# A ViT tower on one core: class attention placed inside the last group's attention, class rows' FFN with its own buffers

## The chip, the cores and the metric

The kernel runs on one core of a Trainium2 chip. Its metric is the device time of one execution in microseconds (us). A core has TensorE (PE, matrix products and transposes, results into PSUM), VectorE (DVE), ScalarE (ACT), GpSimd (POOL) and SyncE (SP, which issues DMAs), each working through its own list of instructions in order; they wait for each other by semaphores.

## The reference

64 images of 3x224x224 become 64 patch tokens of width 128 and one class token each; then one layer of attention and a feed-forward network (FFN) with experts.

```python
tokens = jnp.einsum('bpi,hi->bph', patches, W) + b
h = jnp.concatenate([cls, tokens], axis=1) * pos_embed
# attention on layernorm(h), 8 heads of 16
q = relu(split_heads(x @ Wq.T + bq)); k = relu(split_heads(x @ Wk.T + bk)); v = split_heads(x @ Wv.T + bv)
attn = softmax(einsum('bhnd,bhmd->bhnm', q, k) / (k.sum(-1, keepdims=True) + 1e-6))
h = h + einsum('bhnm,bhmd->bhnd', attn, v) merged @ Wo.T + bo
# FFN on layernorm(h), normalised once more with ln_scale and ln_bias
a, b = split(flat @ shared_in_w.T, 2); out_shared = (silu(a) * b) @ shared_out_w.T + shared_out_b
h_expert = the same form with expert_in_w                      # one hidden vector for all experts
routed = sum over 8 experts of comb[:, e] * (h_expert @ expert_out_weight[e].T)   # group by argmax, top 2 of 4 by softmax
h = h + out_shared + routed
```

## The kernel before

The 64 images are worked in 8 groups of 8 (GROUPS = 8, L = 7 is the last); a group is 512 patch tokens, four tiles of 128. `groups(engine, body)` writes `body(g, par)` for each group on each engine, with a loop over the middle ones. In a body stand the attention of group g, the FFN of group g-1, and, except in the last two groups, the patch embedding of group g+2. The order of the work is written out by hand on each engine: nothing plans it. `need(engine, event, g)` waits until the event of group g has come.

Attention of a group goes in four parts p: `score(g, p)`, `row_maxes`, `exps`, `prob_transpose`, `probs_out`, `prob_v(g, p)`, `row_sums`; then `attn_scale`, `attn_sum`, `attn_transpose`, `attn_out`, `out_proj`, `residual`, `norm2`, `norm2_scale`, `z_transpose`, `z_out`. The FFN of a group goes: `gates`, `logits`, `ffn_in(g, k)` for k = 0 to 3 (k = 0, 1 the shared net, 2, 3 the expert net; each six matmuls of high and low parts), `silus`, `hidden_mul`, `choose` (top 2), `route_exp`, `weights`, `counts`, `shared_t`, `shared_natural`, `shared_add`, and the eight expert products `expert(g, u)`, which `weigh(g, u)` multiplies by the routing weights and GpSimd's `expert_sum` adds up; `output` is the last sum, `store` the DMA to memory. All 64 class tokens of the kernel are one more pass, called group 8 (GROUPS), of 64 rows.

The class tokens' attention over the patches is done once, in the last group: `class_scores`, `class_max`, the exponentials, `class_softmax`, `class_probs`, then `class_values(0)` and `(1)`, 32 matmuls of 8 columns each half, `class_own` and `class_out`. Before the change the value halves stand behind `out_proj` and `z_transpose` of group 7, in banks acc and O, and the class rows' FFN uses the patch rows' tiles (z_nat, z_hi, silu, hidden, comb), so its steps wait until group 7 has finished with them. Behind the last body each engine has a written-out tail with group 7's FFN and the class rows' FFN.

Two waits matter below. `ffn_in(g, 0)` waits for all eight weighings of group g-1, since both use bank C0; and `weigh(g, u)` for even u waits for an earlier `expert_sum`, since there are two product buffers for the four tiles:

```python
if half == 0:
    if t >= 2:
        need(dve, tree_done, g, t - 1)
    else:
        need(dve, tree_done, g - 1, t + 3)
```

## Time and profile before

| | |
|---|---|
| median of 3 runs | 537.16 us (536.97 to 537.72) |
| the profiled execution's own time | 538.47 us |
| its span | 536.6 us |
| TensorE busy | 489.3 us, 91% |
| VectorE, ScalarE, GpSimd busy | 321.2, 184.1, 173.8 us |
| mean granted clock of TensorE | 0.94 of full |

The span is the time between the first and the last instruction of the profiled execution. The views read are: the page; busy time and granted clock by stretch ("PEclk" 1.00 is 2.4 GHz, 0.50 is 1.2 GHz); the timeline of one engine, whose rows give start, duration, engine, line, operation, tiles and what ended an idle time before it; and the chain that ended last. The last group's body runs from about 424 us on, the written-out tail from about 486 us.

### The profile page before, as it was taken

Reading aid. Unit: us, or ns where it says so; the run is one execution under the profiler, and the core shown is the slowest. Engines: PE = TensorE matmul, PEld = TensorE weight load, DVE = VectorE, ACT = ScalarE, POOL = GpSimd, SP = SyncE. Lnnn points to the kernel's source line nnn. Section 1 sums busy time; section 2 is a strip of 40 time slices with the busy share of each in tenths; the row PEclk is TensorE's granted clock in tenths of the full one; section 3 lists DMA queues with packets and bytes.
Section 4 is the critical chain, followed back from the end, with each engine's and each line's share of the span. In section 5 each row is a group of like instructions: output and inputs, shape, how many; then the busy total and the mean of one; then the engine's idle time right before and its main releaser. Section 6 shows DMA issues by size and latency. Waiting matters only on the chain.

```text
span 536.6 us, 6981 instructions
## 1 busy us (share of the span) xinstructions
PE 489.3 (91%) x2194; PEld 331.9 (62%) x2194; DVE 321.2 (60%) x869; ACT 184.1 (34%) x342; POOL 173.8 (32%) x213
## 2 busy tenths in 40 slices
PE   5899997999999999999999999999697869898974
PEld 2355556665775578557755776567576646786562
DVE  0043356375856586658765776667677758646652
ACT  0035115432273218411742255215631553122220
POOL 6013201120462037202711183107311821224443
PEclk9989996899999999999999999999979978969976
DMA  8995660055004600461045200000100010000001
GB/s 340 352 410 188 203 223 0 0 177 184 1 20 165 197 1 6 136 200 41 0 136 164 79 0 20 0 0 1 21 0 1 1 21 0 1 1 1 20 1 22
DMA packets 14413, 44.71 MB, mean 83 GB/s; under 512 B 1721, under 2 KB 7090, under 8 KB 14386
## 3 DMA queue, kind: packets, MB, share of 16 engines
q1 hardware_dynamic: 12882, 42.39, 23.4%
q10 hardware_dynamic: 1504, 1.99, 1.1%
q8 instruction: 14, 0.23, 0.2%
q14 instruction: 13, 0.11, 0.1%
HBM read 42.24 MB, written 2.13 MB: 83 GB/s over the span
## 4 chain that ended last, share of the span: by engine, by line
PE 68%; DVE 15%; issue 7%; DMA 4%; POOL 3%; ACT 2%; ACTq 1%; DVEq 0%; POOLq 0%; SPq 0%
PE acc L421 20%; PE scores L482 6%; PE O L508 5%; PE B L407 4%; DMA bq_row<-in_bq_row 3%; DVE z_nat L1080 2%; PE scores L620 2%; PE C L620 2%; PE B L445 2%; PE C L621 1%; PE acc L655 1%; PE C L559 1%; PE C L622 1%; PE B L464 1%; PE scores L621 1%
## 5 line engine op out<-in xcount | busy, mean ns | idle before, releaser
L421 PE MATMUL acc<-x_main,w_patch 128*128 128x512 f32 x288 | 137.6, 607 | 5.9 <-DMA w_patch<-in_w_patch 5.9
L421 PEld LDWEIGHTS acc<-x_main,w_patch 128*128 128x128 f32 x288 | 53.2, 194 | 49.3 <-issue 41.4
L1567 POOL TENSOR_TENSOR prod<-prod 128x512 f32<-128x512 f32 (+1 forms) x33 | 42.6, 1292 | 35.2 <-DVE prod L1292 35.1
L839 ACT ACTIVATE probs<-shift 128x512 f32<-128x512 f32 x32 | 20.4, 637 | 80.8 <-DVE shift L1132 80.8
L508 PEld LDWEIGHTS O<-v_bd,probs_t 128*128 128x128 f32 x256 | 33.6, 200 | 22.7 <-issue 12.1
L1560 POOL TENSOR_TENSOR hidden_lo<-silu,hidden_hi 128x512 fp32r<-128x512 f32 (+1 forms) x18 | 20.9, 1164 | 74.8 <-ACT hidden_hi L839 74.7
L482 PE MATMUL scores<-k_bd,q_mask 128*128 128x260 f32 x128 | 38.4, 425 | 5.8 <-DVE shift L1132 3.1
L508 PE MATMUL O<-v_bd,probs_t 128*128 128x64 f32 (+1 forms) x256 | 35.6, 284 | 5.0 <-ACT probs_t L839 5.0
L1128 DVE TENSOR_REDUCE row_max<-scores 128x8 f32<-128x520 f32 x32 | 22.3, 698 | 28.8 <-PE scores L482 28.4
L482 PEld LDWEIGHTS scores<-k_bd,q_mask 128*128 128x128 f32 x128 | 23.3, 203 | 18.7 <-issue 7.9
L1529 POOL TENSOR_TENSOR p_cls<-exp_cls,row_rec 128x16 f32<-128x16 f32 x16 | 3.5, 222 | 94.0 <-DVE row_rec L1147 94.0
L839 ACT ACTIVATE probs_t<-B 128x512 f32<-128x512 f32 x32 | 19.0, 593 | 43.3 <-PE B L407 43.3
L620 PE MATMUL C<-w_eout_hi,hidden_hi 128*128 128x512 f32 (+1 forms) x66 | 30.5, 462 | 1.9 <-POOL hidden_lo L1560 0.7
L1292 DVE TENSOR_TENSOR prod<-scores,comb 128x512 f32<-128x512 f32 (+1 forms) x33 | 22.5, 683 | 15.8 <-POOL routed L1574 9.8
L620 PE MATMUL scores<-w_eout_hi,hidden_hi 128*128 128x512 f32 (+1 forms) x66 | 30.0, 454 | 0.2 <-DVE prod L1292 0.2
L1510 POOL TENSOR_TENSOR rstd<-var,neg_half 128x4 f32<-128x4 f32 x8 | 8.1, 1015 | 64.8 <-DVE var L1076 64.8
L1158 DVE TENSOR_TENSOR attn_patch<-O,row_rec 64x256 f32<-64x256 f32 x32 | 13.5, 422 | 25.4 <-PE O L508 24.9
L621 PE MATMUL C<-w_eout_lo,hidden_hi 128*128 128x512 f32 (+1 forms) x66 | 28.4, 430 | 0.0
L622 PE MATMUL C<-w_eout_hi,hidden_lo 128*128 128x512 f32 (+1 forms) x66 | 28.2, 428 | 0.0
L621 PE MATMUL scores<-w_eout_lo,hidden_hi 128*128 128x512 f32 (+1 forms) x66 | 27.7, 420 | 0.0
L622 PE MATMUL scores<-w_eout_hi,hidden_lo 128*128 128x512 f32 (+1 forms) x66 | 27.6, 418 | 0.0
L1292 DVE TENSOR_TENSOR prod<-C,comb 128x512 f32<-128x512 f32 (+1 forms) x33 | 22.0, 679 | 8.9 <-PE C L622 8.9
(251 smaller groups left out, 1016.7 us busy)
## 6 DMA issues: line engine op xcount, KB each, us to landing
x_main<-in_x_main SPq DMA_DIRECT2D x48, 768.0 KB, 4.2
out_tokens<-y_out SPq DMA_DIRECT2D x16, 128.0 KB, 2.5
w_patch<-in_w_patch ACTq DMA_DIRECT2D x6, 192.0 KB, 9.7
prod<-in_w_eout SPq DMA_DIRECT2D x2, 512.0 KB
x_tail<-in_x_tail SPq DMA_DIRECT2D x8, 96.0 KB, 3.3
silu<-in_w_in SPq DMA_DIRECT2D x2, 256.0 KB
hidden<-in_rows ACTq DMA_DIRECT2D x1, 256.0 KB, 16.1
w_attn<-in_w_attn ACTq DMA_DIRECT2D x1, 256.0 KB, 17.5
```

Source lines behind the costliest of these rows:

```text
L407: last = nc.tensor.transpose(dst[0:rows, t * 128:(t + 1) * 128], src, ident)
L421: last = mm(acc[:, :], w_patch[:, j, :], x_main[:, j, :], start=(j == 0), stop=False)
L482: last = mm(scores[:, b2, 0:HP * SEQ], q_mask[:, b, :, :].rearrange("p e n -> p (e n)"), k_bd[:, b, :, :].rearrange("p h m -> p (h m)"), s ...
L508: last = mm(O[:, c:c + 64].rearrange("p (b c) -> p b c", b=2), probs_t[p % 2][:, hp * 128:(hp + 1) * 128], pair, start=True, stop=True)
L620: mm(dst[0:rows, :], h_hi, w_hi, start=(c == 0), stop=False)
L621: mm(dst[0:rows, :], h_hi, w_lo, start=False, stop=False)
L622: last = mm(dst[0:rows, :], h_lo, w_hi, start=False, stop=(c == HC - 1))
L839: return nc.scalar.activation(dst, src, func, **kw)
L1128: v.tensor_reduce(row_max[p % 2][:, :, :], s, AX.X, ALU.max).then_inc(max_done.sem, 1)
L1292: v.tensor_tensor(prod[t % 2][0:rows, half, :].rearrange("p (e d) -> p e d", d=D), src[0:rows, :].rearrange("p (e d) -> p e d", d=D), bcas ...
L1560: q.tensor_tensor(hidden_lo[:, c, 0:n], silu[c][:, 0:n], hidden_hi[:, c, 0:n].bitcast(F32), ALU.subtract).then_inc(hlo_done.sem, 1)
L1567: q.tensor_tensor(p[r, 0, :], p[r, 0, :], p[r, 1, :], ALU.add).then_inc(tree1_done.sem, 1)
```

## The change

The class attention's steps move forward into the last group's attention: `class_max` ahead of `row_maxes(7, 0)`, `class_softmax` ahead of `row_sums(7, 0)`, `class_probs` behind `score(7, 2)`, `class_values(0)` behind `prob_transpose(7, 1)`, `class_values(1)` behind `score(7, 3)`, `class_out` ahead of `prob_v(7, 3)`. The second bank of the values is C0 and not O, for which `shared_t(6)` waits. The expert products of group 6, `counts(6)`, `shared_t(6)` move back accordingly. The class rows' second norm moves into the body, with tiles of its own (h2_cls, z_cls, zc_t, zc_hi, zc_lo, silu_cls, hidden_cls and its high and low part, comb_cls), which end the waits for the patch rows' tiles. In the tail the class FFN stands between group 7's steps, its two expert products go to banks O and acc, VectorE adds them up itself (`class_experts`), they stand ahead of the products 6 and 7 of group 7, and the class rows are stored ahead of group 7's. One of the three table loads of ScalarE in the tail is gone. GpSimd's sums 1 to 3 of group 6 move behind z_low(7) and between the steps of the tail. The memory set aside for DMA descriptors is made smaller, to fit the new tiles.

```diff
                 load_x(g)
-            for g in range(GROUPS - 5, GROUPS):
+            for g in range(GROUPS - 5, GROUPS - 1):
                 store(g)
 
-            need(sp, yout_done, GROUPS)
+            sp.wait_ge(tdve.sem, 22)
             sp.dma_start(out[:, 0, :], y_cls[0:IMAGES, 0:D]).then_inc(stored.sem, 16)
+            store(GROUPS - 1)
...
                 t, half = u // 2, u % 2
-                if u == 0:
+                if is_class(g):
+                    need(pe, hlo_done, g)
+                    need(pe, hid_done, g)
+                elif u == 0:
...
                     need(pe, prod_done, g, u - 3)
-                if isinstance(g, int) and g == GROUPS:
-                    need(pe, prod_done, g - 1)
-                dst = expert_bank(u)
+                dst = (O, acc)[u] if is_class(g) else expert_bank(u)
...
                 score(g, 2)
+                if not nxt:
+                    class_probs()
...
                 fill(9, 10)
-                if lean:
+                if not nxt:
+                    class_values(0)
+                elif lean:
                     expert(g - 1, 0, 128)
                 prob_v(g, 1)
+                score(g, 3)
                 if not nxt:
-                    class_probs()
-                score(g, 3)
+                    class_values(1)
...
                 fill(13, 14)
-                if lean:
+                if not nxt:
+                    expert(g - 1, 0, 128)
+                elif lean:
...
                 fill(18, NMAIN + 1)
-                if lean:
+                if not nxt:
+                    shared_t(g - 1, TOK)
+                    class_out()
+                elif lean:
...
                     to_natural(g + 1, 1 - par)
-                if lean:
+                if not nxt:
+                    shared_natural(g - 1, TILES, 128)
+                    expert(g - 1, 1, 128)
+                elif lean:
...
                     expert(g - 1, 1, 128)
+                if not nxt:
+                    expert(g - 1, 2, 128)
...
                     normed_t(g + 1)
-                else:
-                    class_values(0)
...
                     expert(g - 1, 4, 128)
+                if last:
+                    expert(g - 1, 5, 128)
+                if not nxt:
+                    expert(g - 1, 6, 128)
+                if last:
+                    z_transpose(g)
                 if nxt and last:
-                    expert(g - 1, 5, 128)
-                if last:
-                    z_transpose(g)
-                if not nxt:
-                    class_values(1)
-                    expert(g - 1, 5, 128)
-                if last:
                     expert(g - 1, 6, 128)
+                if last:
...
             L = GROUPS - 1
+            need(pe, z_done, GROUPS, 1)
+            need(pe, zt_done, L)
+            nc.tensor.transpose(B1[:, 0:IMAGES], z_cls[0:IMAGES, :], ident[0:IMAGES, 0:IMAGES])\
+                .then_inc(zt_full.sem, 1)
             gates(L, TILES, 128)
-            class_out()
-            for k in range(4):
-                ffn_in(L, k, TOK)
-            counts(L, TILES, 128)
-            shared_t(L, TOK)
-            need(pe, z_done, GROUPS, 1)
-            nc.tensor.transpose(B1[:, 0:IMAGES], z_nat[0:IMAGES, 0:128], ident[0:IMAGES, 0:IMAGES])\
-                .then_inc(zt_full.sem, 1)
-            expert(L, 0, 128)
+            ffn_in(L, 0, TOK)
+            ffn_in(L, 1, TOK)
             gates(GROUPS, 1, IMAGES)
-            shared_natural(L, TILES, 128)
-            for u in range(1, 4):
-                expert(L, u, 128)
+            ffn_in(L, 2, TOK)
+            ffn_in(L, 3, TOK)
             ffn_in(GROUPS, 0, IMAGES)
             ffn_in(GROUPS, 1, IMAGES)
-            expert(L, 4, 128)
-            expert(L, 5, 128)
+            shared_t(L, TOK, (0,))
+            expert(L, 0, 128)
+            counts(L, TILES, 128)
+            expert(L, 1, 128)
+            shared_t(L, TOK, (1,))
             ffn_in(GROUPS, 2, IMAGES)
             ffn_in(GROUPS, 3, IMAGES)
+            expert(L, 2, 128)
+            shared_natural(L, TILES, 128)
+            expert(L, 3, 128)
+            expert(L, 4, 128)
             counts(GROUPS, 1, IMAGES)
-            expert(L, 6, 128)
             shared_t(GROUPS, IMAGES)
-            expert(L, 7, 128)
+            expert(L, 5, 128)
...
             expert(GROUPS, 1, IMAGES)
+            expert(L, 6, 128)
+            expert(L, 7, 128)
...
                 exps(g, 0)
+                if not nxt:
+                    act.wait_ge(tdve.sem, 4)
+                    go(tc_exp[:, :, :], tc_shift[:, :, :], ACT.Exp).then_inc(tact.sem, 1)
+                    go(tc_cc_exp[:, :], tc_cc[:, :], ACT.Exp).then_inc(tact.sem, 1)
...
                 probs_out(g, 0)
+                if last:
+                    hidden_high(g - 1, 1, TOK)
                 if not nxt:
-                    act.wait_ge(tdve.sem, 4)
-                    go(tc_exp[:, :, :], tc_shift[:, :, :], ACT.Exp).then_inc(tact.sem, 1)
-                    go(tc_cc_exp[:, :], tc_cc[:, :], ACT.Exp).then_inc(tact.sem, 1)
-                if last:
-                    hidden_high(g - 1, 1, TOK)
+                    act.wait_ge(tpe.sem, 2)
+                    go(tc_prob_t[:, :], acc[:, 256:512]).then_inc(tact.sem, 1)
+                if last:
...
                 probs_out(g, 1)
-                if not nxt:
-                    act.wait_ge(tpe.sem, 2)
-                    go(tc_prob_t[:, :], acc[:, 256:512]).then_inc(tact.sem, 1)
...
             L = GROUPS - 1
+            z_out(GROUPS, IMAGES)
...
                 silus(L, k, TOK)
-            load_table(L, 3, ACT.Exp)
-            counts_out(L, TOK)
             hidden_high(L, 0, TOK)
             hidden_high(L, 1, TOK)
+            silus(GROUPS, 0, IMAGES)
+            silus(GROUPS, 1, IMAGES)
+            counts_out(L, TOK)
+            silus(GROUPS, 2, IMAGES)
+            silus(GROUPS, 3, IMAGES)
+            load_table(L, 3, ACT.Exp)
             route_exp(L, TILES, 128)
             shared_out(L, TOK)
-            z_out(GROUPS, IMAGES)
-            route_exp(GROUPS, 1, IMAGES)
-            load_table(L, 4, ACT.Silu)
-            for k in range(4):
-                silus(GROUPS, k, IMAGES)
             hidden_high(GROUPS, 0, IMAGES)
             hidden_high(GROUPS, 1, IMAGES)
+            route_exp(GROUPS, 1, IMAGES)
...
                     hidden_mul(g - 1, 3, TOK)
+                if not nxt:
+                    class_max()
...
                 if not nxt:
-                    class_max()
+                    class_softmax()
...
                 row_sums(g, 1)
-                if not nxt:
-                    class_softmax()
...
                 attn_sum(g, 0)
+                if not nxt:
+                    class_own()
...
                 attn_sum(g, 1)
+                if not nxt:
+                    class_residual()
...
                     weigh(g - 1, 0, 128)
+                if not nxt:
+                    weigh(g - 1, 1, 128)
                 residual(g, par)
                 norm2(g, h2[par], TILES, 128)
-                if last:
+                if nxt and last:
                     weigh(g - 1, 1, 128)
+                elif not nxt:
+                    weigh(g - 1, 2, 128)
                 norm2_scale(g, h2[par], TILES, 128)
-                if last:
+                if not nxt:
+                    weigh(g - 1, 3, 128)
+                    norm2(GROUPS, h2_cls, 1, IMAGES)
+                    weigh(g - 1, 4, 128)
+                    norm2_scale(GROUPS, h2_cls, 1, IMAGES)
+                    for u in range(5, 2 * TILES):
+                        weigh(g - 1, u, 128)
+                elif last:
                     for u in range(2, 2 * TILES):
                         weigh(g - 1, u, 128)
-                        if not nxt and u == 4:
-                            class_own()
...
             logits(L, TILES, 128)
-            choose(L, TILES, 128)
             hidden_mul(L, 0, TOK)
             hidden_mul(L, 1, TOK)
-            dve.wait_ge(tpe.sem, 4)
-            v.tensor_tensor(h2[0][0:IMAGES, 0:D], acc[0:IMAGES, 128:256], h_cls_bo[0:IMAGES, :], ALU.add)\
-                .then_inc(h2_done.sem, 1)
             hidden_mul(L, 2, TOK)
             hidden_mul(L, 3, TOK)
-            norm2(GROUPS, h2[0], 1, IMAGES)
-            norm2_scale(GROUPS, h2[0], 1, IMAGES)
+            choose(L, TILES, 128)
+            output(L - 1, TILES, 128)
+            hidden_mul(GROUPS, 0, IMAGES)
+            hidden_mul(GROUPS, 1, IMAGES)
             weights(L, TILES, 128)
-            output(L - 1, TILES, 128)
-            shared_add(L, h2[1], TILES, 128)
             weigh(L, 0, 128)
             weigh(L, 1, 128)
+            hidden_mul(GROUPS, 2, IMAGES)
+            hidden_mul(GROUPS, 3, IMAGES)
             logits(GROUPS, 1, IMAGES)
+            weigh(L, 2, 128)
+            shared_add(L, h2[1], TILES, 128)
             choose(GROUPS, 1, IMAGES)
-            weigh(L, 2, 128)
             weigh(L, 3, 128)
             weights(GROUPS, 1, IMAGES)
-            hidden_mul(GROUPS, 0, IMAGES)
-            hidden_mul(GROUPS, 1, IMAGES)
             weigh(L, 4, 128)
-            hidden_mul(GROUPS, 2, IMAGES)
-            hidden_mul(GROUPS, 3, IMAGES)
             weigh(L, 5, 128)
+            shared_add(GROUPS, h2_cls, 1, IMAGES)
+            class_experts()
             weigh(L, 6, 128)
             weigh(L, 7, 128)
-            shared_add(GROUPS, h2[0], 1, IMAGES)
-            weigh(GROUPS, 0, IMAGES)
-            weigh(GROUPS, 1, IMAGES)
             output(L, TILES, 128)
-            output(GROUPS, 1, IMAGES)
...
                 norm_scale2(g, TILES, 128)
-                if last:
+                if last and nxt:
                     for t in range(TILES - 1):
                         expert_sum(g - 1, t, 128)
+                elif last:
+                    expert_sum(g - 1, 0, 128)
+                    norm_scale2(GROUPS, 1, IMAGES)
                 z_low(g, TOK)
-                if last:
+                if last and nxt:
...
             L = GROUPS - 1
-            norm_scale2(GROUPS, 1, IMAGES)
+            expert_sum(L - 1, 1, 128)
+            z_low(GROUPS, IMAGES)
+            expert_sum(L - 1, 2, 128)
             hidden_low(L, 0, TOK)
             hidden_low(L, 1, TOK)
-            z_low(GROUPS, IMAGES)
+            expert_sum(L - 1, 3, 128)
             expert_sum(L, 0, 128)
-            expert_sum(L, 1, 128)
             hidden_low(GROUPS, 0, IMAGES)
             hidden_low(GROUPS, 1, IMAGES)
+            expert_sum(L, 1, 128)
             expert_sum(L, 2, 128)
             expert_sum(L, 3, 128)
-            expert_sum(GROUPS, 0, IMAGES)
```

On TensorE, in the attention of group 7: from the third score to the third product of probabilities and values. Before:

```order
L482 MATMUL scores<-k_bd,q_mask 128x260 x2
L407 MATMUL B<-const,probs 128x128 x4
L620 MATMUL C<-w_eout_hi,hidden_hi 128x512
...
L508 MATMUL O<-v_bd,probs_t 128x64 x4
L642 MATMUL acc<-const,x_main 128x128 x2
L482 MATMUL scores<-k_bd,q_mask 128x260 x2
L574 MATMUL B<-const,count 9x128 x4
```

Now, where each "..." stands for the rest of the 32 matmuls of a half of the class values:

```order
L511 MATMUL scores<-k_bd,q_mask 128x260 x2
L676 MATMUL acc<-const,x_main 128x128 x2
L436 MATMUL B<-const,probs 128x128 x4
L689 MATMUL acc<-tc_prob_t,v_bd 128x8
...
L537 MATMUL O<-v_bd,probs_t 128x64 x4
L511 MATMUL scores<-k_bd,q_mask 128x260 x2
L689 MATMUL acc<-tc_prob_t,v_bd 128x8
...
L693 MATMUL C<-tc_pcc_bd,v_cls_rows 128x64
L604 MATMUL B<-const,count 9x128 x4
```

The two halves of class values came in, the expert product of group 6 went out, and the counts stand behind the second half.

On GpSimd, at the end of the last body (rstd is the power of `norm_scale2`, prod and routed the three steps of a sum, z_lo is `z_low`). Before:

```order
L1514 TENSOR_TENSOR rstd<-var,neg_half 128x4
L1567 TENSOR_TENSOR prod<-prod 128x512
L1569 TENSOR_TENSOR prod<-prod 128x256
L1574 TENSOR_TENSOR routed<-prod 128x128
L1567 TENSOR_TENSOR prod<-prod 128x512
L1569 TENSOR_TENSOR prod<-prod 128x256
L1574 TENSOR_TENSOR routed<-prod 128x128
```

Now:

```order
L1599 TENSOR_TENSOR rstd<-var,neg_half 128x4
L1655 TENSOR_TENSOR prod<-prod 128x512
L1657 TENSOR_TENSOR prod<-prod 128x256
L1662 TENSOR_TENSOR routed<-prod 128x128
L1599 TENSOR_TENSOR rstd<-var,neg_half 64x1
L1642 TENSOR_TENSOR z_lo<-z_t,z_hi 128x512
L1655 TENSOR_TENSOR prod<-prod 128x512
L1657 TENSOR_TENSOR prod<-prod 128x256
```

The class rows' power and z_lo of group 7 stand ahead of the second sum.

On ScalarE, in the tail, from the last silu of group 7 on. Before:

```order
L839 ACTIVATE silu<-scores 128x512
L839 ACT_TABLE_LOAD
L839 ACTIVATE table_row<-const 128x1
L839 ACTIVATE count_t<-B 9x512
L839 ACTIVATE hidden_hi<-silu 128x512 x2
L839 ACTIVATE e_exp<-e_shift 128x32
L839 ACTIVATE hn_t<-C 128x512
```

Now:

```order
L889 ACTIVATE silu<-scores 128x512
L889 ACTIVATE hidden_hi<-silu 128x512 x2
L889 ACTIVATE silu_cls<-O 128x64
L889 ACTIVATE silu_cls<-acc 128x64
L889 ACTIVATE count_t<-B 9x512
L889 ACTIVATE silu_cls<-O 128x64
L889 ACTIVATE silu_cls<-acc 128x64
L889 ACT_TABLE_LOAD
L889 ACTIVATE table_row<-const 128x1
L889 ACTIVATE e_exp<-e_shift 128x32
L889 ACTIVATE hn_t<-C 128x512
```

The four class silus and the counts came ahead of the table load, and with it ahead of the exponential of the routing (e_exp) and the copy of the shared product (hn_t).

## Rows read from the trace of the kernel before

**Rows 1.** The page: span; busy time by engine; chain that ended last, by engine.

```profile
span 536.6 us, 6981 instructions
...
PE 489.3 (91%) x2194; PEld 331.9 (62%) x2194; DVE 321.2 (60%) x869; ACT 184.1 (34%) x342; POOL 173.8 (32%) x213
...
PE 68%; DVE 15%; issue 7%; DMA 4%; POOL 3%; ACT 2%; ACTq 1%; DVEq 0%; POOLq 0%; SPq 0%
```

**Rows 2.** Stretches: length, busy PE, PEld, DVE, ACT, POOL, clock, DMA share, GB/s.

```profile
437.40:447.20 9.80, 7.59 (x25) 6.21 (x26) 7.19 (x20) 3.71 (x10) 2.56 (x2) 0.50 0.01 2
447.40:464.70 17.30, 14.71 (x82) 10.53 (x80) 12.60 (x38) 5.22 (x11) 1.98 (x6) 1.00 0.00 0
464.70:467.70 3.00, 3.00 (x56) 2.95 (x54) 2.70 (x13) 0.00 (x0) 0.22 (x1) 1.00 0.02 5
...
468.90:474.60 5.70, 5.70 (x16) 4.41 (x17) 3.85 (x7) 0.00 (x0) 3.85 (x5) 0.50 0.00 0
...
511.90:515.00 3.10, 0.00 (x0) 0.00 (x0) 2.89 (x10) 0.00 (x0) 2.43 (x3) 1.00 0.00 0
515.70:529.00 13.30, 12.64 (x37) 8.90 (x37) 3.28 (x8) 1.18 (x6) 5.55 (x8) 0.50 0.01 1
```

**Rows 3.** Timeline of PE, class values: start, duration, line, tiles.

```profile
464.75 0.27 PE L655 MATMUL acc<-tc_prob_t,v_bd 64*128 64x8 f32 x1
...
467.68 0.25 PE L655 MATMUL acc<-tc_prob_t,v_bd 64*128 64x8 f32 x1
...
468.21 0.36 PE L655 MATMUL acc<-tc_prob_t,v_bd 64*128 64x8 f32 x1
...
468.43 0.36 PE L655 MATMUL acc<-tc_prob_t,v_bd 64*128 64x8 f32 x1
```

**Rows 4.** Timeline of PE, attention of group 7: score, shared product, probabilities times values.

```profile
444.33 2.05 PE L482 MATMUL scores<-k_bd,q_mask 128*128 128x260 f32 x4
...
452.92 1.02 PE L585 MATMUL C<-hidden,w_sout 128*128 128x512 f32 x2
...
454.73 1.12 PE L589 MATMUL C<-count_t,out_bias 9*128 9x512 f32 x2
...
459.02 1.00 PE L508 MATMUL O<-v_bd,probs_t 128*128 128x64 f32 x8
```

**Rows 5.** Timeline of PE: z transposes, first FFN matmul, first expert product, last matmul.

```profile
474.22 0.80 PE L407 MATMUL B<-const,z_nat 128*128 128x128 f32 x4
...
487.56 0.50 PE L559 MATMUL C<-z_hi,w_in_hi 128*128 128x512 f32 x1
...
500.23 0.51 PE L620 MATMUL C<-w_eout_hi,hidden_hi 128*128 128x512 f32 x1 [0.70 <-POOL hidden_lo L1560]
...
529.82 0.39 PE L622 MATMUL scores<-w_eout_hi,hidden_lo 128*64 128x512 f32 x1
```

**Rows 6.** Timeline of DVE: residual, normalised tiles, first step of choose, first hidden product.

```profile
464.86 0.69 DVE L1178 TENSOR_TENSOR h<-B,h_nat 128x512 f32<-128x512 f32 x1 [1.27 <-PE B L524]
...
468.53 2.88 DVE L1080 TENSOR_SCALAR z_nat<-h,mv,rstd 128x128 f32<-128x128 f32 x4 [0.54 <-POOL rstd L1514]
...
487.54 0.98 DVE L1212 TENSOR_TENSOR g_sel<-g_logit 128x4 f32<-128x4 f32 x1
...
491.37 0.68 DVE L1268 TENSOR_TENSOR hidden<-silu,C 128x512 f32<-128x512 f32 x1
```

**Rows 7.** Timelines of POOL (first and last step of a sum) and ACT (table load).

```profile
472.69 1.28 POOL L1567 TENSOR_TENSOR prod<-prod 128x512 f32<-128x512 f32 x1 [1.62 <-DVE prod L1292]
...
474.85 0.45 POOL L1574 TENSOR_TENSOR routed<-prod 128x128 f32<-128x128 f32 x1
...
495.12 1.28 ACT L839 ACT_TABLE_LOAD   x1
```

**Rows 8.** Chain that ended last: start, duration, what; a store from output to landing.

```profile
501.44 0.69 DVE y_out L1300
...
502.79 2.45 DMA out_tokens<-y_out
```

133 lines of the change are left out of this document (93 added, 40 removed).

## The prediction

> **What bounds the kernel now.** The page comes first: TensorE is busy 91% of the span and the chain of waits runs through it for 68%, VectorE 15%, "issue" 7% [rows 1]. So a step counts by what TensorE does, or waits for, while it runs. The change touches nothing before about 435 us, the place where the last group's (group 7's) attention starts; I read only the last 100 us, by stretches with their granted clock, and then each engine's timeline.
>
> In the stretches the reader should see the clock. It is full (2.4 GHz) where TensorE streams wide operands, and half (1.2 GHz) in four places: 437.4 to 447.2, when scores wait for VectorE; twice right behind the small matmuls of the class values, of which 468.9 to 474.6 is one; and 515.7 to 529.0, after a gap of 3.1 us with nothing on TensorE [rows 2]. The third place matters most. Through 464.7 to 467.7 TensorE had no idle time at all and ran class value matmuls of 8 columns; then the clock fell. A pair of them (one matmul record into each of two banks) starts every 0.11 at full clock (27 pairs from 464.75 to 467.68) and every 0.21 at half [rows 3].
>
> **The change part by part**, as a walk along the engines; times are us of the profiled span.
>
> *Up to 447.* Class maximum moves ahead of the first row maximum, into VectorE time that was idle: a gain of about 1.2 there. Class softmax (1.7) now stands ahead of the third row maximum, which costs it 0.6. TensorE goes on as before until 446.4, then does the class probability transposes (0.5) and those of the second pair (0.9), to 447.7. In 437.4 to 447.2 TensorE was busy 7.6 of 9.8 us, its idle time early, and then the clock came back [rows 2]; the late part of it is as busy as before, so I take it to come back again.
>
> *The two halves of the class values.* They were behind the out projection; now they stand before the second and behind the fourth score, expert product 0 having made room. A half is 32 pairs. First half: 447.7, 27 pairs at 0.11 until the clock falls as it did after 3.0 us [rows 2, 3], 5 at 0.21: done at 451.8. Probabilities times values, 1.0 at full clock and so 2.0 at half, to 453.8; a score, 2.05 at half clock and 0.1 of it overlapped, to 455.7 [rows 4]. Second half wholly at half clock: 32 x 0.21 = 6.8, and the class rows' 0.6, to 463.1. No work on this path hides them: attention of the last group waits on TensorE's order. The next releases of ScalarE (the third exponentials are queued behind the copy of the counts, and the counts stand behind the class values) come after 464.
>
> *Rest of attention.* Counts, transposes (0.8 at half clock [rows 5]), expert product 0 (5.3 us for two at half clock, 2.65 for one, from 468.9 to the row at 474.22 [rows 2, 5]; at full clock I take 1.4): 467.6. I let the clock return here, after a stretch with wide work throughout. Then values 1.0, transposes 0.5, the shared product 2.9 (from 452.92 to 455.85 [rows 4]), class out projection 0.4: 472.5. The last copy of probabilities is queued on ScalarE behind the copy of the shared product, both after 472.1, so the last values run 473.3 to 474.4. They ended at 460.0 before [rows 4]: **14.4 late.** From there the chain (scale, sum, transposes, copy, an expert product, out projection) is 5.3 to 479.7, and from the residual to the last normalised tile it took 464.86 to 471.41, 6.5 [rows 6]: 486.3. Expert products 3 to 6 lie beside this. The transposes of group 7's z start at 486.4 where they were at 474.22 [rows 5]: 12.2 late. In exchange the second class half (4.2) and all but one of the late expert products are gone from behind them.
>
> *A new wait.* GpSimd now does only the first of group 6's expert sums there, then the class power, then z_lo, and the second sum after that. z_lo starts when ScalarE has written z (about 488.5) and takes 1.3; a sum takes from 472.69 to 475.30, 2.6 [rows 7]; so the second sum is done at 492.4. VectorE's weighing of product 6 writes the buffer that this sum reads and waits for it; queued behind it are weighing 7, group 7's logits, and with them the first FFN matmul, which needs bank C0. Two weighings (0.68 each [rows 6]) and the logits: FFN starts at 494.0. Before it was 487.56 [rows 5]: **6.4 late.** TensorE has only the class transpose and the gates in 488.4 to 494, so the clock is half as after the gap before 515 [rows 2]: I take half until 498.5, which costs 2.1.
>
> *FFN of group 7.* The four steps, with the class rows' first two (1.4) between, end at 503.4; expert product 0 waits for GpSimd's hidden_lo until 505.3. Before: 500.23 [rows 5]. **5.1 late.** Choosing the experts (3.8, from 487.54 to 491.37 [rows 6]) has moved behind the hidden products: the 1.5 that TensorE idled for it goes. After that the class rows' FFN, which stood at the end, fills places. But ScalarE loads the exponential table (1.28 [rows 7]) only behind the last class silu (512.3), then route_exp (514.0), then the copy of the shared product. VectorE's weights (1.4) wait for route_exp, and behind these stand two weighings, class steps, a third weighing and the shared sum at 518.4, for which expert product 3 waits. TensorE idles 513.5 to 514.7 and 515.1 to 518.4 and is at half clock until 522.4. Then eight products' worth of work to 531.5; the end was 530.2 [rows 5]. **1.3 late.**
>
> *The end.* Before, the class rows' sum on GpSimd and its short store came last: 6.4 from the last matmul to 536.6. Now VectorE does the class sum (1.8) ahead of the last two weighings, which so end at 532.5 and not 532.2; the fourth sum 2.6, the output 0.7, and the store of group 7 with its two issues, 3.1 from the end of the output sum (502.13) to the landing (505.24) [rows 8]: 538.9.
>
> The sum on the span: 536.6 + 1.3 (last matmul) + 1.0 (longer end) = **538.9**. The profiled execution took 538.47 with what lies around its span, so 540.8 for such a one; the median of the runs shown is 537.16, 1.31 below the profiled one, so I predict **539.5**. The chip's memory setting and the separate buffers add no instruction; I take zero, and see no row that bounds them but the unchanged loads.
>
> **A rule weighed against the trace.** The rows show the clock falling behind class values without idle time ahead of the fall. The Trainium skill (TensorE: Matmul & The Clock Gate, Why this matters for your kernels) advises to keep idle gaps between bursts of matmuls short to avoid drops. By that rule filling the attention's gaps with class values would hold the full clock; the trace disagrees at 467.8, and the first rival below prices that outcome from rows.
>
> **The rivals.** *Faster: class values among wider matmuls keep the clock full.* For it: attention at full clock held it from 447.4 to 464.7 with 2.6 us idle [rows 2]. Against: the first half alone is 3.5 us of 8-column matmuls, the length after which it fell. It decides at about 451. The price: half one to 451.2, values and score to 453.3, VectorE's row maximum meanwhile, half two to 457.2, shared product done at 464.0 and not 472.1: 8.1 less, **531.4**. *Faster, smaller: the new wait on GpSimd's second sum and the wait behind the table load don't bite.* That takes away 3.0 + 2.1 at most at the first, less what expert product 0 waits anyway, and up to 3.3 at the second: about 4 in all, **535.5**. For it: a walk adds waits that real slack may swallow. Against: both are hard orders in a queue. *Slower: the clock does not come back at 447 since 0.5 of transposes more stand in place of an expert product, and comes back later after 464.* The first half then is 6.8, not 4.1 (2.7), and values and shared product lose 1.6: **543.8**. *It does not do what it says:* the class rows' chain still sets the end, if their weights are late: 2 more at the end, inside the forecast's own range, 537.5 to 542.
>
> **How the numbers follow.** Forecast 0.55, full clock 0.13, waits that don't bite 0.12, clock low for longer 0.20. Predicted is the forecast's 539.5. Leaving out the full-clock case and the far end of the slow one gives 532.5 to 544.5. A run of this kernel can tell about 0.2% (1.1 us) from no change. Faster: 0.13 + 0.11 and 0.01 of the forecast, 0.25. Within 0.2% (536.1 to 538.2): 0.14 of the forecast and 0.01, 0.15. Slower: 0.60.
>
> **What would show it.** Half clock from about 451 to 467; last values of the attention near 474; z transposes near 486; TensorE nearly idle before an FFN start near 494, VectorE waiting there for GpSimd; a gap of some 3 us before expert product 3 near 515; last matmul near 531 and group 7's store as the last work. If the clock is full at 455, the walk is wrong from there and the kernel is faster. If the FFN starts within 2 us of the z transposes, the new wait was no wait.

## The result, and the profile after

The changed kernel is slower by more than was forecast, and outside the range.

| | before | changed |
|---|---|---|
| median (lowest to highest) of 4 runs each | 537.07 us (536.65 to 537.72) | 545.96 us (543.91 to 546.87) |
| ratio, 95% interval | 1 | 1.0159 [1.0135, 1.0182] |
| the profiled execution's own time, its span | 538.47, 536.6 us | 543.91, 542.1 us |

All ratios here are of fast runs: on two of the chips they leave out the runs of the kernel before that took over 1.5% more than its fastest (6 of 19 and 4 of 25), and so they can lie up to 0.4% from the quotient of the medians given.

The page of the changed kernel: span, busy times, and the shares of the chain that ended last.

```profile
span 542.1 us, 6976 instructions
...
PE 489.0 (90%) x2194; PEld 333.2 (61%) x2194; DVE 321.4 (59%) x872; ACT 182.5 (34%) x340; POOL 170.7 (31%) x210
...
PE 68%; DVE 13%; issue 7%; POOL 4%; DMA 3%; ACT 2%; ACTq 1%; DVEq 0%; POOLq 0%
```

TensorE was busy as long as before (489.0 us to 489.3, [rows 1]); the longer span is idle time, 5.8 us more of it. So the page doesn't say where it is. The stretches do (window, length, busy PE, PEld, DVE, ACT, POOL, granted clock, DMA share, GB/s):

```profile
434.70:442.40 7.70, 3.76 (x21) 2.92 (x22) 6.08 (x17) 3.98 (x11) 1.79 (x2) 1.00 0.01 2
442.90:466.50 23.60, 23.60 (x163) 21.56 (x162) 12.53 (x39) 3.42 (x9) 1.22 (x4) 0.50 0.00 1
...
476.90:494.00 17.10, 11.97 (x62) 9.28 (x60) 12.47 (x35) 4.23 (x7) 9.15 (x11) 1.00 0.01 2
494.10:497.30 3.20, 3.20 (x8) 2.52 (x9) 0.22 (x1) 0.60 (x1) 1.08 (x2) 0.50 0.00 0
...
514.70:524.60 9.90, 6.67 (x18) 4.59 (x17) 7.54 (x29) 2.17 (x7) 3.51 (x6) 0.50 0.01 2
524.80:534.50 9.70, 9.01 (x41) 6.05 (x39) 6.89 (x17) 0.44 (x2) 4.28 (x6) 1.00 0.00 0
```

Against [rows 2] the reader should see one thing. Before, the attention ran from 447.4 to 464.7 at full clock. Now 442.9 to 466.5 is one piece at half clock, and TensorE has no idle time in it at all. The timeline of PE has the landmarks of [rows 4, 5]: last attention values, z transposes, first FFN matmul, first expert product, counts, expert product 3.

```profile
472.46 1.10 PE L537 MATMUL O<-v_bd,probs_t 128*128 128x64 f32 x8 [0.81 <-ACT probs_t L889]
...
486.39 0.66 PE L436 MATMUL B<-const,z_nat 128*128 128x128 f32 x4 [1.07 <-DVE z_nat L1133]
...
504.87 0.50 PE L654 MATMUL C<-w_eout_hi,hidden_hi 128*128 128x512 f32 x1 [0.87 <-POOL hidden_lo L1648]
508.52 0.60 PE L604 MATMUL B<-const,count 128*9 128x128 f32 x4 [1.99 <-DVE count L1288]
...
520.40 0.79 PE L654 MATMUL C<-w_eout_hi,hidden_hi 128*128 128x512 f32 x1 [2.97 <-DVE y_out L1332]
```

The first FFN matmul stands at 494.05, after 2.77 idle; VectorE's timeline shows what it waited for, a weighing that itself waits 1.98 for GpSimd's sum, the logits behind it. This is the new wait that the prediction named:

```profile
492.53 0.69 DVE L1348 TENSOR_TENSOR prod<-scores,comb 128x512 f32<-128x512 f32 x1 [1.98 <-POOL routed L1662]
493.14 0.68 DVE L1348 TENSOR_TENSOR prod<-C,comb 128x512 f32<-128x512 f32 x1
493.74 0.15 DVE L1252 TENSOR_TENSOR g_logit<-C,gate_b 128x8 f32<-128x8 f32 x1
```

The last matmul ends at 534.21. VectorE's last weighing follows at 534.45, GpSimd's last sum at 535.21 to 537.8, VectorE's output to 538.6, and group 7's store lands at 542.1: the last work, as predicted.

### The profile page after: what moved, and what is told of

The parts are those of the page before. It is cut to its first block, busy times and chain, and to the rows that moved or that the text cites. A ratio compares the mean times of both kernels' runs of the same rounds, so it can differ in the third digit from the quotient of the medians.

```text
span 542.1 us, 6976 instructions
## 1 busy us (share of the span) xinstructions
PE 489.0 (90%) x2194; PEld 333.2 (61%) x2194; DVE 321.4 (59%) x872; ACT 182.5 (34%) x340; POOL 170.7 (31%) x210
## 3 DMA queue, kind: packets, MB, share of 16 engines
q10 hardware_dynamic: 1504, 1.99, 1.1%
## 4 chain that ended last, share of the span: by engine, by line
PE 68%; DVE 13%; issue 7%; POOL 4%; DMA 3%; ACT 2%; ACTq 1%; DVEq 0%; POOLq 0%
PE acc L450 20%; PE scores L511 6%; PE O L537 6%; PE B L436 4%; DMA bq_row<-in_bq_row 3%; PE acc L689 2%; DVE z_nat L1133 2%; PE C L589 2%; PE B L474 1%; DVE stats L1115 1%; PE C L590 1%; PE C L591 1%; PE B L493 1%; POOL rstd L1599 1%; PE scores L589 1%
## 5 line engine op out<-in xcount | busy, mean ns | idle before, releaser
L1655 POOL TENSOR_TENSOR prod<-prod 128x512 f32<-128x512 f32 x32 | 41.1, 1283 | 29.0 <-DVE prod L1348 29.0
L1648 POOL TENSOR_TENSOR hidden_lo<-silu,hidden_hi 128x512 fp32r<-128x512 f32 x16 | 20.2, 1267 | 77.9 <-ACT hidden_hi L889 77.9
L654 PE MATMUL C<-w_eout_hi,hidden_hi 128*128 128x512 f32 x64 | 28.6, 447 | 3.8 <-DVE y_out L1332 3.0
L1348 DVE TENSOR_TENSOR prod<-scores,comb 128x512 f32<-128x512 f32 x32 | 21.8, 683 | 13.0 <-POOL routed L1662 11.8
L654 PE MATMUL scores<-w_eout_hi,hidden_hi 128*128 128x512 f32 x64 | 28.5, 445 | 0.2 <-DVE prod L1348 0.2
L656 PE MATMUL scores<-w_eout_hi,hidden_lo 128*128 128x512 f32 x64 | 26.6, 416 | 0.0
L656 PE MATMUL C<-w_eout_hi,hidden_lo 128*128 128x512 f32 x64 | 26.5, 415 | 0.0
L655 PE MATMUL C<-w_eout_lo,hidden_hi 128*128 128x512 f32 x64 | 26.5, 414 | 0.0
L655 PE MATMUL scores<-w_eout_lo,hidden_hi 128*128 128x512 f32 x64 | 26.3, 411 | 0.0
L1657 POOL TENSOR_TENSOR prod<-prod 128x256 f32<-128x256 f32 x32 | 25.1, 786 | 2.5
## 6 DMA issues: line engine op xcount, KB each, us to landing
w_attn<-in_w_attn ACTq DMA_DIRECT2D x1, 256.0 KB, 17.1
```

The source lines that it names most:

```text
L654: mm(dst[0:rows, :], h_hi, w_hi, start=(c == 0), stop=False)
L655: mm(dst[0:rows, :], h_hi, w_lo, start=False, stop=False)
L656: last = mm(dst[0:rows, :], h_lo, w_hi, start=False, stop=(c == HC - 1))
L1348: v.tensor_tensor(prod[t % 2][0:rows, half, :].rearrange("p (e d) -> p e d", d=D), src[0:rows, :].rearrange("p (e d) -> p e d", d=D), bcas ...
L1655: q.tensor_tensor(p[r, 0, :], p[r, 0, :], p[r, 1, :], ALU.add).then_inc(tree1_done.sem, 1)
L1657: q.tensor_tensor(p[r, 0, 0:2 * D], p[r, 0, 0:2 * D], p[r, 0, 2 * D:4 * D], ALU.add)\
```

## The experiments

Times of the kernel before differ from execution to execution (532.4 to 543.1 us over the chips used here), so each ratio is to runs of it on the same chip, and a difference of two experiments is read from ratios only where their intervals lie apart. Otherwise the verdict rests on the waits in the traces. Positions of single landmarks move with the clock too, so stretches between two landmarks are compared rather than positions.

**The changed kernel again**, on another chip, with no edit, to see what is fixed and what varies.

> The changed kernel once more, beside the three kernels that differ from it in one part. Theory (waits): the same landmarks in the trace as in the first one: z transposes of group 7 at 486.4, first FFN matmul of group 7 at 494.1, expert product 3 at 520.4, last matmul at 533.6, span 542 to 545. Rival (the granted clock): the times of the other executions, up to 3 us above the first profiled one, come from other places of the half clock, so the landmarks move with it by 1 us or more while the waits named stay.

Measured: 544.42 us, ratio 1.014 [1.0053, 1.0228]. The two waits that the prediction named were the same (2.78 us ahead of the first FFN matmul, 3.01 ahead of expert product 3), and choose took as long; the counts waited 0.91 and not 1.99. The half clock was not at the same places: 436.5 to 446.5 and 450 to 467 in the attention, and 504.5 to 511.5, 515 to 518.5 and 521.5 to 525 in the tail. The landmarks moved with it, as the rival said: z transposes at 485.07 (1.3 earlier), first FFN matmul at 492.72, expert product 3 at 521.47 (1.1 later), last matmul ending at 534.90. So the waits belong to the order of the work, and the clock's places to the execution. Here the clock did what the prediction had said: it was back at 446.5, and the class values ran at full clock until it fell at 450. A pair starts every 0.11 us up to there and every 0.21 behind it:

```profile
446.79 0.27 PE L689 MATMUL acc<-tc_prob_t,v_bd 64*128 64x8 f32 x1
...
450.07 0.36 PE L689 MATMUL acc<-tc_prob_t,v_bd 64*128 64x8 f32 x1
...
450.29 0.36 PE L689 MATMUL acc<-tc_prob_t,v_bd 64*128 64x8 f32 x1
```

**GpSimd's second sum first.** All of what the class rows put between the first two sums moves behind them.

```diff
                     expert_sum(g - 1, 0, 128)
-                    norm_scale2(GROUPS, 1, IMAGES)
+                    expert_sum(g - 1, 1, 128)
                 z_low(g, TOK)
...
             L = GROUPS - 1
-            expert_sum(L - 1, 1, 128)
+            norm_scale2(GROUPS, 1, IMAGES)
             z_low(GROUPS, IMAGES)
```

(VectorE's class norm scale, the class transpose and ScalarE's z_out follow it, between the first FFN steps.)

> One edit to the changed kernel: GpSimd does the second sum of group 6 ahead of z_low of group 7; the class rows' power, their normalised tile, its transposes and copies go behind it. Theory (GpSimd's order makes VectorE wait): the first FFN matmul of group 7 comes at about 491 and not 494.1, and the kernel is 2.5 to 4 us faster than the changed one. Rival (that wait covers another, or only the clock counts): FFN start moves, the end does not, under 1 us.

Measured: 542.23 us, ratio 1.0117 [1.0035, 1.0199]. The z transposes stood at 486.19, as in the changed kernel, and the FFN began at 491.94 and not 494.05. In its PE timeline the wait ahead of the FFN is down from 2.77 to 0.84:

```profile
490.06 1.03 PE L568 MATMUL C<-w_gate,z_t 128*128 128x10 f32 x8 [1.60 <-DVE prod L1350]
491.94 0.68 PE L589 MATMUL C<-z_hi,w_in_hi 128*128 128x512 f32 x1 [0.84 <-DVE e_logit L1255]
```

From the z transposes to the first FFN matmul it took 5.75 us, and 7.65 in both traces of the changed kernel: the wait was real, and worth about 2 us there. The medians on this chip differ by as much (542.23 and 544.42), though the intervals of the ratios overlap; 2.5 to 4 had been expected.

**The routing exponential early.** ScalarE loads the table and takes the exponential ahead of the counts' copy, at the price of two more table loads.

```diff
             silus(GROUPS, 1, IMAGES)
+            load_table(L, 3, ACT.Exp)
+            route_exp(L, TILES, 128)
+            load_table(L, 4, ACT.Silu)
             counts_out(L, TOK)
             silus(GROUPS, 2, IMAGES)
             silus(GROUPS, 3, IMAGES)
-            load_table(L, 3, ACT.Exp)
-            route_exp(L, TILES, 128)
             shared_out(L, TOK)
+            load_table(L, 5, ACT.Exp)
```

> One edit to the changed kernel: ScalarE loads the exponential table and does the routing exponential of group 7 ahead of the counts' copy and of the last two class silus, and copies the shared product right behind those; two table loads (1.28 us each) are added. Theory (the routing exponential is late behind the class silus and the table load, and VectorE's weights and the shared sum behind it): expert product 3 comes about 3.4 us earlier than 520.4, the kernel is 3 to 5 us faster than the changed one. Rival (the added table loads only move the wait): under 1 us.

Measured: 541.36 us, ratio 1.0094 [1.0058, 1.0129]. TensorE's wait ahead of expert product 3:

```profile
519.32 0.80 PE L654 MATMUL C<-w_eout_hi,hidden_hi 128*128 128x512 f32 x1 [0.78 <-DVE y_out L1334]
```

0.78 and not 2.97: the second wait that the prediction named was real too, again 2 us. From expert product 0 to product 3 it took 12.9 us (506.46 to 519.32), in the changed kernel 15.5 (504.87 to 520.40), and 17.1 in its repeat, where half clock fell into that stretch. The ratio lies apart from that of the changed kernel's first runs (1.0159 [1.0135, 1.0182]).

**Each half of the change alone.** First the tail alone (lines against the kernel before): class attention stays where it was, and the class rows have their own buffers and run between the tail's steps, but their first two FFN steps only behind expert product 0. Then the body alone (lines against the changed kernel), with the tail's steps in the order of before.

```diff
             class_out()
-            for k in range(4):
-                ffn_in(L, k, TOK)
-            counts(L, TILES, 128)
-            shared_t(L, TOK)
+            ffn_in(L, 0, TOK)
+            ffn_in(L, 1, TOK)
+            ffn_in(L, 2, TOK)
+            ffn_in(L, 3, TOK)
+            shared_t(L, TOK, (0,))
...
```

> One half of the change alone: the class attention stays where it was before (value halves behind the out projection and behind the z transposes, banks acc and O), GpSimd's sums of group 6 too; only the class rows' FFN has buffers of its own and runs between the steps of group 7's FFN. Theory (the move of the class values into the attention costs the time): z transposes at 474.3 and FFN start at 487.6 as before the change, and the end 2 to 6 us before the kernel before, ratio 0.989 to 0.997. Rival (the interleaved tail costs it): the same FFN start, but the end 3 us or more above the kernel before, ratio over 1.005.

Measured: 536.19 us, ratio 0.9991 [0.9945, 1.0037]: no difference, neither the gain of the theory nor the loss of the rival. The FFN began at 486.25 and the wait ahead of expert product 3 was 3.43 (VectorE's y_out), even longer than in the changed kernel, because ScalarE's exponential is behind the class silus here too.

```diff
             logits(L, TILES, 128)
-            hidden_mul(L, 0, TOK)
...
             choose(L, TILES, 128)
-            output(L - 1, TILES, 128)
-            hidden_mul(GROUPS, 0, IMAGES)
-            hidden_mul(GROUPS, 1, IMAGES)
+            for k in range(4):
+                hidden_mul(L, k, TOK)
             weights(L, TILES, 128)
+            output(L - 1, TILES, 128)
+            shared_add(L, h2[1], TILES, 128)
...
```

> The other half of the change alone: the last group's body as in the changed kernel (class attention inside, GpSimd's sums behind), but the tail in the order of the kernel before, on the new buffers; VectorE adds up the class rows at the end. Theory (the body costs the time, the tail gives a little back): first FFN matmul of group 7 near 494, last matmul near 537, the kernel 6 to 9 us above the one before, no better than the changed kernel. Rival (the interleaved tail with its late routing exponential costs it): 1 to 3 us below the changed kernel, since TensorE would not wait 3 us for expert product 3.

Measured: 541.32 us, ratio 1.0066 [1.0021, 1.0111]: slower than before, by 3.5 us where 6 to 9 had been expected. Two rows of its PE timeline, the FFN start and the class rows' third FFN step, which in the old order of the tail waits alone for the class rows' first hidden product:

```profile
490.88 0.80 PE L589 MATMUL C<-z_hi,w_in_hi 128*128 128x512 f32 x1 [4.24 <-DVE e_logit L1246]
...
519.12 0.30 PE L589 MATMUL O<-zc_hi,w_in_hi 128*128 128x64 f32 x1 [3.18 <-DVE hidden_cls L1317]
```

By the ratios the halves alone (+0.7% and no change) are less than the whole (+1.4 to +1.6%), though the ends of the intervals touch. In the profiled executions, expert product 0 came at 500.23 before [rows 5], 495.17 with the tail alone, 504.33 with the attention alone, 504.87 with both; from there to the end it took 36.4, 36.8, 34.5 and 37.2. These positions hold the clock too: up to the z transposes the attention alone and the whole change have the same order on TensorE, and yet they stood at 483.24 and 486.39. From the z transposes to expert product 0 it took 26.0 before, 22.1 with the tail alone, 21.1 with the attention alone and 18.5 with both (19.3 in the repeat). So ahead of expert product 0 the tail's order saves 3.9 us on the old attention and 1.8 to 2.6 on the moved one. Behind it, to the end, the tail's order costs 0.4 us on the old attention and 2.7 to 3.9 on the moved one (the repeat took 38.4). GpSimd's late sums of group 6 stand in that last part; how much of it is theirs and how much the clock's, these single executions don't separate.

**The class values left out in either place.** In each half, the class value matmuls of 15 of the 16 image pairs are left out, so the class rows' result is missing from what these two kernels compute.

```diff
-                for pair in range(16 * half, 16 * half + 16):
+                for pair in range(16 * half + 15, 16 * half + 16):
```

> The changed kernel without 30 of the 32 pairs of class value matmuls (the class rows' result is left out by that), all waits kept: the price of these matmuls inside the attention. Theory (they lengthen the attention and bring the half clock): 6.8 + 4.1 us of matmuls and 2 to 5 us of half clock go, the z transposes come at 472 to 476 and not 486.4, the kernel is 9 to 14 us faster than the changed one. Rival (the attention is late by the order of the other steps, such as the counts' copy ahead of the third exponentials): z transposes at 480 or later, under 6 us gained.

> The kernel before without the same 30 of 32 pairs (class rows' result left out): the price of the same matmuls behind the attention. Theory: there they took 8.3 us of TensorE's time and left half clock for the expert products behind them, about 5 us: 10 to 13 us faster than the kernel before, so that the place of the matmuls changes their price by little, and what the move costs is the wait of everything behind the attention. Rival (behind the attention they fill idle time): under 7 us, and the move makes them dearer by 4 us or more.

Measured: from the changed kernel 536.69 us, ratio 0.9973 [0.9933, 1.0013]; from the kernel before 529.39 us, ratio 0.9834 [0.9758, 0.9911]. So the values cost 1.66% (8.9 us; 0.9 to 2.4% by the interval, and 8.0 us by the medians) in the old place, between what theory and rival had said, and 1.67 to 1.86% (9 to 10 us, from the two ratios of the changed kernel) in the new. The old place didn't hide them, and the new one doesn't either. And a difference of 7.3 us between the two kernels is there without the values. The stretches of the changed kernel without values:

```profile
449.00:456.00 7.00, 7.00 (x27) 5.50 (x26) 5.04 (x16) 1.69 (x4) 0.16 (x1) 0.51 0.00 0
456.00:462.50 6.50, 5.44 (x25) 2.92 (x24) 2.73 (x8) 1.08 (x2) 0.98 (x3) 1.00 0.00 0
```

and of the kernel before without them:

```profile
445.50:468.50 23.00, 17.74 (x96) 12.66 (x95) 17.46 (x54) 5.21 (x11) 4.60 (x9) 1.00 0.00 1
```

With the values the half clock lasted 23.6 us, without them 7.0, then it came back. (In the eight traces with the values inside the attention its long stretch there lasted 14 to 24 us, so its length varies too.) In the old order there was none at all between 445.5 and 468.5. The z transposes stood at 476.09 and 469.77: of the 7.3 us, 6.3 are there by then. So it is the order of the other steps, and the half clock that goes with it: this pair of experiments doesn't separate them, the next one takes out a part of the order.

**Values of the last pair first.** The fourth pair's values stand ahead of the shared product on TensorE, and its probabilities' copy ahead of the shared product's copy on ScalarE (the lines below); expert product 2 moves behind the out projection.

```diff
                 probs_out(g, 2)
-                if lean:
+                if lean and nxt:
                     shared_out(g - 1, TOK)
...
                 probs_out(g, 3)
+                if not nxt:
+                    shared_out(g - 1, TOK)
```

> One edit to the changed kernel: in the last attention part the probabilities times values stand ahead of the shared product of group 6 (and the copy of the last probabilities ahead of the copy of the shared product); the shared product then fills the wait for the scaling, and an expert product the wait for the copy of the attention. Class values stay in the attention. Theory (a part of the lateness is the order of the other steps there, not the class values): z transposes at about 483 and not 486.4, the kernel 2 to 3 us faster than the changed one. Rival (the attention is bound by TensorE's work ahead of it): under 1 us.

Measured: 541.94 us, ratio 1.0068 [1.0036, 1.01]. The last values stood at 466.33, 6.1 earlier than in the changed kernel, and the z transposes at 480.78, 5.6 earlier:

```profile
464.20 1.00 PE L537 MATMUL O<-v_bd,probs_t 128*128 128x64 f32 x8
466.33 1.10 PE L537 MATMUL O<-v_bd,probs_t 128*128 128x64 f32 x8 [0.69 <-ACT probs_t L891]
```

Not all of that is the edit's: the last class value stood at 459.81 and not 462.40, so 2.6 us were there ahead of the edited place, with half clock for 14 us instead of 23.6. From the last class value to the last attention values it took 6.5 us, and 10.1 in the changed kernel (10.9 in its repeat); to the z transposes 21.0, and 24.0 and 23.9. So the edit gains 3.0 us, as the theory said, since the shared product leaves the path.

**The mends together**: GpSimd's sum first with the exponential early, and then all three.

> The changed kernel with both earlier repairs: GpSimd's second sum ahead of z_low, and the routing exponential ahead of the class silus. Theory (two waits one behind the other): the gains add up, 5 to 6 us, to within 2 us of the kernel before. Rival (the end is bound by something else, such as the class rows' sum on VectorE ahead of the last weighings): about 3 us, as the second repair alone.

> The changed kernel with all three repairs, class values still inside the attention. Theory (the values between the attention's parts cost their own time and more, wherever the waits are mended): at the time of the kernel before or up to 2 us under it, and 3 us or more slower than the repaired tail with the class attention behind (532.2). Rival (with the waits gone the values inside are as good as behind): within 1.5 us of that kernel.

Measured: 539.03 us, ratio 1.0032 [0.9992, 1.0071], and 538.0 us, ratio 0.9991 [0.9963, 1.0019]. Against the 1.0159 [1.0135, 1.0182] of the changed kernel both intervals lie apart; against its repeat (1.014 [1.0053, 1.0228]) only that of all three does. With all three the change is worth nothing: no difference from the kernel before. The half clock in the attention of all three is as long as in the changed kernel (14 us with two):

```profile
445.00:469.00 24.00, 24.00 (x165) 21.82 (x164) 12.74 (x39) 3.42 (x9) 1.41 (x5) 0.50 0.00 1
```

**The tail alone, mended.** Class attention stays as before; on ScalarE the exponential and the shared copy come early, on VectorE the weights, and the class rows' own sum stands behind the last weighing. (Lines against the tail alone; the shared sum on VectorE also moves ahead by two places, and on TensorE steps of the shared products change places with an expert product three times.)

```diff
+            load_table(L, 3, ACT.Exp)
+            route_exp(L, TILES, 128)
+            load_table(L, 4, ACT.Silu)
             counts_out(L, TOK)
...
             choose(L, TILES, 128)
+            weights(L, TILES, 128)
             output(L - 1, TILES, 128)
...
             weigh(L, 7, 128)
+            class_sum()
             output(L, TILES, 128)
```

> The tail half alone (class attention as in the kernel before, own buffers, class FFN between), with the routing exponential of group 7 and the copy of the shared product ahead of the last class silus, the weights ahead of the class rows' hidden products, and the adding up of the class rows behind the last weighing. Theory (in that tail the wait for expert product 3 is the largest one): it goes from 3.4 us to under 1, last matmul 3 us or more before that of the tail half (524.1), the kernel 3 to 5 us faster than the tail half and 1 percent faster than the kernel before. Rival (two more table loads and GpSimd's sums take its place): within 1 us of the tail half.

> The repaired tail with the class attention where it was before, once more, on the same chip as the kernel with all three repairs: ratio to the kernel before 0.985 to 0.993. If it were a matter of the chip or of the clock's phase, the ratio would come out over 0.995.

Measured: 532.22 us, ratio 0.9875 [0.9787, 0.9964], and again on another chip 531.03 us, ratio 0.987 [0.9809, 0.9931]. It is faster than both kernels, and on the chip of the three mends 7.0 us faster than those (531.03 and 538.00); the two differ in the tail as well as in the place of class attention, so this isn't the price of the place alone. Behind the counts no wait of TensorE is over 0.5 us. VectorE's timeline of the first of these shows the weights right behind choose:

```profile
500.56 0.19 DVE L1274 TENSOR_TENSOR count<-e_row,g_sel 128x32 f32<-128x32 f32 x1
500.79 0.19 DVE L1290 TENSOR_TENSOR e_keep<-e_exp,count 128x32 f32<-128x32 f32 x1
...
502.10 0.19 DVE L1300 TENSOR_TENSOR comb<-e_keep,e_den 128x32 f32<-128x32 f32 x1
```

## Why the prediction was right in its path and short in its sum

| step | predicted | profiled execution |
|---|---|---|
| class values start | 447.7 | 445.1 |
| clock | full to 450.7, half to 467.8 | half 442.9 to 466.5 |
| last values | 473.3 to 474.4 | 472.46 to 473.5 |
| z transposes | 486.4 | 486.39 |
| first FFN matmul | 494.0 | 494.05 |
| expert product 0 | 505.3 | 504.87 |
| expert product 3 | 518.4 | 520.40 |
| last matmul ends | 531.5 | 534.21 |
| end of span | 538.9 | 542.1 |
| median | 539.5 | 545.96 |

**Up to expert product 0: within half a microsecond from the z transposes on**, though for this execution the attention's clock was told wrongly. The second score and the first values came at full clock, so the class values started 2.6 earlier, then everything ran at half clock. Two errors cancelled. That the clock returned at 447 was taken from the similar stretch of before; in the profiled execution it had fallen only at 442.9. The last values stood 0.8 ahead of the walk for that, and the chain from their end to the end of the out projection took that back (6.2 us and not 5.3). So agreement to a tenth at the z transposes is luck: in the six traces whose TensorE has the same order up to there they stood between 483.2 and 488.0. The walk's clock itself was a possible one, since the repeat had it (full from 446.5 to 450, half to 467).

**The first rival fell.** A clock kept full by class values between wider matmuls didn't happen; 23.60 us at 0.50 with no idle time is its opposite. The rule of the Trainium skill that was weighed (TensorE: Matmul & The Clock Gate, Why this matters for your kernels), to keep gaps short, fits the fall at 442.9, behind a stretch with 3.76 us busy of 7.70 and gaps of up to 2.35; it doesn't tell that the clock then stays low through 23.6 us without a gap. The second rival (waits that don't bite) fell with the waits of 2.77 and 2.97. The rival of a clock that is low for longer gave the number nearest to the result, 543.8, and its condition was met, no full clock at 447. But its price didn't come: the full clock ahead of 442.9 had paid for it, and the z transposes were not late.

**The step that failed first: choose at 3.8.** The number came from 487.54 to 491.37 [rows 6]. Moved behind the hidden products it took 5.9 (502.51 to 508.38), so that the counts on TensorE waited 1.99. VectorE's rows in the changed kernel:

```profile
502.51 1.10 DVE L1268 TENSOR_TENSOR g_sel<-g_logit 128x4 f32<-128x4 f32 x1
503.65 1.19 DVE L1269 TENSOR_SCALAR g_sel<-g_sel 128x4 f32<-128x4 f32 x1
504.87 0.19 DVE L1270 TENSOR_REDUCE e_max<-e_logit 128x8 f32<-128x32 f32 x1
505.09 1.02 DVE L1272 TENSOR_TENSOR e_shift<-e_logit,e_max 128x32 f32<-128x32 f32 x1
...
506.35 0.70 DVE L1278 TENSOR_TENSOR e_ge<-e_ge,const 128x128 f32<-128x128 f32 x1
```

and GpSimd's beside them:

```profile
502.33 2.49 POOL L1648 TENSOR_TENSOR hidden_lo<-silu,hidden_hi 128x512 fp32r<-128x512 f32 x2 [7.07 <-ACT hidden_hi L889]
504.77 1.30 POOL L1655 TENSOR_TENSOR prod<-prod 128x512 f32<-128x512 f32 x1
506.15 0.76 POOL L1657 TENSOR_TENSOR prod<-prod 128x256 f32<-128x256 f32 x1
```

An operation on four elements of a partition takes 1.19 us, and ends (504.84) when GpSimd's instruction ends (504.82). The one at 505.09 ends at 506.11, GpSimd's at 506.07; the one at 506.35 at 507.05, GpSimd's at 506.91. The Trainium skill (SBUF — State Buffer, SBUF: two separate sides) says that VectorE and GpSimd lock a port pair for a whole instruction, where VectorE's uses both ports, or reads two inputs from SBUF beside a GpSimd instruction that reads SBUF, and that the one that started second waits in full. By that rule such a step of choose pays for a GpSimd instruction that is already running; the ends in these rows agree. The profile before had it too: the first step of choose took 0.98 from 487.54 [rows 6], to 488.52, and this instruction of GpSimd ended at 488.50:

```profile
487.22 1.28 POOL L1567 TENSOR_TENSOR prod<-prod 128x512 f32<-128x512 f32 x1
```

That row was there to be asked why. Choose ran 4.7 with the tail alone, where GpSimd has but one short instruction (0.32 us) after hidden_lo:

```profile
492.63 2.49 POOL L1621 TENSOR_TENSOR hidden_lo<-silu,hidden_hi 128x512 fp32r<-128x512 f32 x2 [0.83 <-ACT hidden_hi L874]
...
509.25 1.27 POOL L1628 TENSOR_TENSOR prod<-prod 128x512 f32<-128x512 f32 x1 [13.84 <-DVE prod L1332]
```

There the two steps beside hidden_lo took 1.11 and 1.19 us as in the changed kernel, and the two that met a sum in the changed kernel (1.02 and 0.70) were short:

```profile
495.40 0.19 DVE L1256 TENSOR_TENSOR e_shift<-e_logit,e_max 128x32 f32<-128x32 f32 x1
...
495.83 0.29 DVE L1262 TENSOR_TENSOR e_ge<-e_ge,const 128x128 f32<-128x128 f32 x1
```

So choose stretches by what GpSimd does beside it: of the 2.1 us, 0.8 come from its new place beside hidden_lo and 1.2 from the sum moved into the tail. No run changes GpSimd's work and nothing else, so the lock as the reason rests on these rows and on the page.

**Behind it, terms of a few tenths.** The 2.1 went through whole: counts, class silus, table load, exponential, weights, weighings, product 3 at 520.40, 2.0 late on the walk. ScalarE's timeline shows the chain that the prediction told, with the load behind the last class silu:

```profile
513.92 0.23 ACT L889 ACTIVATE silu_cls<-acc 128x64 f32<-128x64 f32 x1 [0.45 <-PE acc L591]
514.17 1.28 ACT L889 ACT_TABLE_LOAD   x1
...
515.57 0.21 ACT L889 ACTIVATE e_exp<-e_shift 128x32 f32<-128x32 f32 x1
```

"Eight products' worth" was 0.7 short, with the half clock ending at 524.6 and not 522.4, and the end 0.5 short (7.9 from the last matmul and not 7.4).

**The median.** The walk gave 540.8 for a profiled execution; it took 543.91, 3.1 more. For the median the prediction took 1.31 off, as in the runs of before; of the changed kernel the profiled execution was the fastest of four, 2.05 under the median. That is 3.4 more, the larger half of the miss of 6.5. The step that failed is "1.31 below the profiled one": a difference between executions was carried over as if it belonged to the program. In the other runs the profiled execution lay 0.2 above its median (the repeat), 1.1 above (exponential early) and 2.4 below (tail alone). The same holds for the prediction's 0.2% for what a run can tell: the kernel before spread over 2%.

Much of such spread goes with the clock. In 63 executions of the kernel before, those with a mean granted clock of 0.956 or more took 532.4 to 534.1 us, those with 0.937 or less 540.0 to 543.1. But it isn't shown to make these 2 us: of the changed kernel's four executions, two with the same mean clock of 0.937 took 543.91 and 545.98. Only one execution of each run has a trace, so the cause of that difference stays open.

Together: of the 6.5 us, choose is 2.1 (of which 2.0 are left at product 3), the products behind product 3 are 0.7, the end 0.5, and the step from the profiled execution to the median 3.4.

**What it was worth beyond the walk.** The class values cost 8 to 10 us wherever they stand. The z transposes are 12.2 late with them and 6.3 late where both kernels leave them out; the tail won some of that back, and lost two waits of 3 us. The prediction had these, in its sum of single steps, except what choose pays beside GpSimd.

## What to carry to other kernels

Work that no idle time of the bounding engine covers cost about the same here in its new place, and delayed the chain that it was moved ahead of: ask for the gap it fills before moving it. When small VectorE operations move, look at what GpSimd runs beside them there, and price them from rows that had the same neighbour. Move the work, then walk each in-order queue for what now stands ahead of the first thing that others wait for; here two such places (a sum, a table load) cost about 2 us each, and the tail alone with its queues mended was the fastest version tried. And a landmark that agrees in one execution is no proof: run the same kernel again and compare stretches between landmarks.

## What the hardware showed that was not expected

- TensorE stayed at half clock for 23.60 us, all of it busy, while narrow class value matmuls stood among wider ones; with 15 of every 16 of them left out it was at half for 7.00 us and came back. In a second execution of the same kernel it was full for 3.5 us among them first, and then at half for 17.00 us, again all busy.
- VectorE operations of 0.15 to 0.3 us took 0.7 to 1.2 us, and ended within 0.15 us of the GpSimd instruction beside them, while reductions between them took 0.19.
- The kernel before, on one core of one chip, took from 533.0 to 542.3 us over 25 runs, with a mean granted clock of 0.956 in the fastest and of 0.933 in the slowest. That spread is as large as what the class values cost in all.
